# Displacement stage: two buffers of x, the factor in the bank, sums of weights spread, POOL adds the tiles of x

## The reference

```
x = x + mamba(ln_c(x))                      # layer 0
t = to_tokens(x); t = t + ffn(ln_t(t)); x = from_tokens(t)
x = x + displace_and_smooth(ln_c(x), offset) # layer 1
t = to_tokens(x); t = t + ffn(ln_t(t)); x = from_tokens(t)

ln_c(v)  = (v - mean over channels) / sqrt(variance over channels + 1e-6)
ffn(x)   = bitlinear(gelu(bitlinear(x, W1, b1)), W2, b2)
bitlinear: each of 5 groups of rows of W becomes sign(W - mean of the group);
           y is scaled by 128 / (max |y| + 1e-5) for each image and clipped; only the first 5 of 8 images are kept
```

## Time and profile before

| | |
|---|---|
| median of 3 runs | 3997.6 us (3991.24 to 4003.83) |
| the profiled execution | 3997.12 us, its span 3995.3 us |
| PE busy | 3294.7 us, 82% of the span |
| DVE busy | 3593.4 us, 90% |
| ACT busy | 2429.6 us, 61% |
| POOL busy | 2658.3 us, 67% |
| mean granted clock of TensorE | 0.84 |
| displacement, first L1185 to first matmul of the next layer | 3392.03 to 3600.58 us |

### The profile page before, as it was taken

The page is one execution under the profiler, slowest core; times in us unless marked ns, Lnnn a source line. Parts: engine busy times, 40 slices in busy tenths (PEclk is TensorE's granted clock), DMA queues, the critical chain, the costliest instruction groups (busy, mean ns, idle before and its releaser), DMA issues. The chain is left out here.

```text
span 3995.3 us, 46643 instructions
## 1 busy us (share of the span) xinstructions
PE 3294.7 (82%) x12666; PEld 2070.6 (52%) x12666; DVE 3593.4 (90%) x3917; ACT 2429.6 (61%) x4147; POOL 2658.3 (67%) x2119
## 2 busy tenths in 40 slices
PE   5878878787878778787878888788768999788998
PEld 2444444445444444444444444445436777456776
DVE  4999999999999999999999999999957888786786
ACT  4766575676667566655756575676535564575653
POOL 3898988989798888888898988989921110253110
PEclk7878878796878878687878878797779999898999
DMA  3020211202020211202020211202030113452112
GB/s 139 9 101 21 97 61 50 93 17 94 17 100 17 101 51 59 94 17 93 17 101 17 101 43 67 93 17 85 16 103 17 51 62 117 168 189 79 49 49 80
DMA packets 81582, 275.28 MB, mean 69 GB/s; under 512 B 15212, under 2 KB 24044, under 8 KB 64900
## 3 DMA queue, kind: packets, MB, share of 16 engines
q1 hardware_dynamic: 80516, 270.82, 18.5%
q10 hardware_dynamic: 768, 1.05, 0.1%
HBM read 229.90 MB, written 41.95 MB: 68 GB/s over the span
## 5 line engine op out<-in xcount | busy, mean ns | idle before, releaser
L644 POOL TENSOR_TENSOR slot<-dtu,b_rep 128x512 f32<-128x512 f32 x1536 | 1908.3, 1274 | 125.2 <-PE ysum L350 125.0
L350 PE MATMUL ysum<-ident,slot 128*128 128x128 f32 x6144 | 1091.1, 327 | 468.9 <-DVE slot L735 258.3
L535 ACT ACTIVATE state<-dt,aneg 128x512 f32<-128x512 f32 x1536 | 1046.1, 689 | 538.3 <-DVE slot L735 503.0
L350 PEld LDWEIGHTS ysum<-ident,slot 128*128 128x128 f32 x6144 | 854.9, 168 | 930.4 <-DVE slot L735 429.0
L735 DVE TENSOR_TENSOR slot<-state,c_rep 128x512 f32<-128x512 f32 x1248 | 839.0, 673 | 0.0
L727 DVE TENSOR_TENSOR_SCAN state<-state,carry,slot 128x512 f32<-128x512 f32 x624 | 792.3, 1280 | 3.6 <-ACT state L535 3.4
L727 DVE TENSOR_TENSOR_SCAN state<-state,slot 128x512 f32<-128x512 f32 x624 | 755.8, 1221 | 37.8 <-ACT state L535 37.8
L654 POOL TENSOR_TENSOR slot<-slot,c_rep 128x512 f32<-128x512 f32 x288 | 366.1, 1271 | 246.0 <-ACT carry L544 158.0
L544 ACT ACTIVATE carry<-state 128x1 f32<-128x1 f32 x624 | 103.1, 165 | 315.7 <-DVE slot L735 314.9
L1282 ACT ACTIVATE hid<-ph_l,bias_l 128x512 f32<-128x512 f32 x240 | 165.0, 691 | 207.5 <-PE ph_l L1080 206.2
L1080 PE MATMUL ph_l<-xh,w 128*128 128x512 f32 x720 | 216.5, 410 | 31.6 <-DVE xl L1506 11.3
(11 more groups left out here) (214 smaller groups left out, 4975.6 us busy)
## 6 DMA issues: line engine op xcount, KB each, us to landing
b_rep<-rows_of_b_and_c SPq DMA_DIRECT2D x64, 1024.0 KB, 4.7
c_rep<-rows_of_b_and_c SPq DMA_DIRECT2D x64, 1024.0 KB, 4.6
xres_l<-between_layers SPq DMA_DIRECT2D x18, 1536.0 KB, 10.1
xn_l<-between_layers SPq DMA_DIRECT2D x17, 1536.0 KB, 8.5
between_layers<-y SPq DMA_DIRECT2D x10, 1536.0 KB, 6.3
xn<-in_x SPq DMA_DIRECT2D x16, 768.0 KB, 4.4
xres<-in_x SPq DMA_DIRECT2D x16, 768.0 KB, 4.5
between_layers<-xres SPq DMA_DIRECT2D x16, 768.0 KB, 3.5
```

Source lines behind the costliest of these rows:

```text
L350: last = mm(ysum[:, cols], slot[:, (NS * k + n) % SLOTS, cols], ident[:], start=n == 0 and j == 0, stop=n == NS - 1, is_transpose=True, sk ...
L535: af(state[:, (NS * k + n) % BANKS], dt[:, k], ACT.Exp, scale=aneg[:, k, n:n + 1]).then_inc(exp_done, 1)
L644: tt(slot[:, q % SLOTS], dtu[:, k % 2], b_rep[:, n], ALU.mult).then_inc(dbu_done, 1)
```

## The change

1. **Two buffers of x.** `xd` is `xn` for even d and a new place `xn_d` for odd d. `load_d(d)` waits for the centring of d-2, not of d-1. The load of image 1 is issued in the last feed-forward image, once its place is free, and that of image 2 right behind it; the load of W2 moves from in front of them to behind the store of the last feed-forward result.
2. **The factor in the bank.** Exp writes its result into `ph[h]` instead of `rstd`, and `scale_of_d` reads it there. The next mean waits for the scaling (`normed_d`) where it waited for Ln.
3. **Sums of weights spread.** The ten group sums go one by one into d = 1, 2 and 3, behind the centring; the means are made in d = 4; the signs go into d = 4, 5 and 6, behind `read_y`.
4. **POOL adds the three tiles of x.** A new function `sum_tiles_d` on POOL adds the tiles into `xsum_d`, and a mean takes one matmul per half (four records instead of twelve).
5. The mean of image 1 moves from behind the ninth down step of the last feed-forward image to behind the twelfth, and `center_of_d(1)` behind `result_largest`.

```diff
+SUM_IN = ((), (0, 1, 2), (3, 4, 5), (6, 7, 8, 9), (), (), (), ())
+TOTAL_IN = 4
+SIGN_IN = ((), (), (), (), (0, 1, 2), (3, 4, 5, 6), (7, 8, 9), ())
...
+        xsum_d = (xsum[0], put("xsum_d", [P, HW], "shared", 19 * TILE // 2))
...
+        xd = (xn, put("xn_d", [P, CT, HW], "shared", NMAT * (P + 2 * SIDE) * 4))
...
             def load_d(d):
                 if d == 0:
                     sp.wait_ge(split_lo, HALVES * FFN_B)
+                elif d == 1:
+                    sp.wait_ge(down_full, DOWNS - AHEAD + 1)
+                    nc.sync.sem_inc(top_seen, 1)
+                    sp.wait_ge(mean_d, HALVES)
                 else:
-                    sp.wait_ge(centered_d, HALVES * d)
+                    sp.wait_ge(centered_d, HALVES * (d - 1))
...
-            sp.wait_ge(down_full, DOWNS)
-            load_w2(1)
+            load_d(1)
             load_d(2)
             spread_top(LAST[0])
             finish(LAST[0])
             sp.dma_start(xres[:], X[MOVED[0]]).then_inc(xres_in_d, 16)
             for d in range(B):
+                if d == 0:
+                    sp.wait_ge(down_full, DOWNS)
+                    load_w2(1)
                 if d + 3 <= B:
                     load_d(d + 3)
...
             def mean_of_d(d):
-                pe.wait_ge(x_in_d, 16 * (d + 1))
...
-                    pe.wait_ge(ln_read_d, HALVES * d)
+                    pe.wait_ge(normed_d, HALVES * d)
...
+                pe.wait_ge(x_summed_d, d + 1)
                 for h in range(HALVES):
-                    for t in range(CT):
-                        last = mm(ph[h][:], mean_w[:], xn[:, t, half(h)], start=t == 0, stop=t == CT - 1)
-                    last.then_inc(mean_d, 1)
+                    mm(ph[h][:], mean_w[:], xsum_d[d > 0][:, half(h)], start=True, stop=True).then_inc(mean_d, 1)
...
-                    r = rstd[:, half(h)]
-                    af(r, r, ACT.Exp, scale=-0.5).then_inc(rstd_d, 1)
+                    af(ph[h][:], rstd[:, half(h)], ACT.Exp, scale=-0.5).then_inc(rstd_d, 1)
...
                     v.tensor_tensor(xc[:, :, half(h)], xc[:, :, half(h)],
-                                    rstd[:, half(h)].unsqueeze(1).broadcast_to([P, CT, T]), ALU.mult).then_inc(normed_d, 1)
+                                    ph[h][:].unsqueeze(1).broadcast_to([P, CT, T]), ALU.mult).then_inc(normed_d, 1)
...
+            def sum_tiles_d(d):
+                pool.wait_ge(x_in_d[d % 2], 16 * (d // 2 + 1))
+                if d == 0:
+                    pool.wait_ge(mean_full, HALVES * FFN_B)
+                elif d == 1:
+                    pool.wait_ge(down_full, DOWNS)
+                else:
+                    pool.wait_ge(mean_d, HALVES * d)
+                o, a = xsum_d[d > 0], xd[d % 2]
+                tt(o[:], a[:, 0], a[:, 1], ALU.add).then_inc(sum_step_d, 1)
+                pool.wait_ge(sum_step_d, d + 1)
+                tt(o[:], o[:], a[:, 2], ALU.add).then_inc(x_summed_d, 1)
...
+            sum_tiles_d(0)
             pool.wait_ge(up_full, UPS)
             nc.gpsimd.memset(mats[:], 0.0).then_inc(mats_zero, 1)
+            sum_tiles_d(1)
             for d in range(B):
+                if d + 2 <= B:
+                    sum_tiles_d(d + 2)
                 add_moved(d)
```

More of the change, by code:

```diff
@@ L914, in layers @@
         step, tapped, gauss = sem("step"), sem("tapped"), sem("gauss")
-        x_in_d, xres_in_d, stored_d = sem("x_in_d"), sem("xres_in_d"), sem("stored_d")
+        x_in_d, xres_in_d, stored_d = [sem(f"x_in_d{j}") for j in range(2)], sem("xres_in_d"), sem("stored_d")
+        sum_step_d, x_summed_d = sem("sum_step_d"), sem("x_summed_d")
         mean_d, centered_d, squared_d, var_d = sem("mean_d"), sem("centered_d"), sem("squared_d"), sem("var_d")
@@ L1371, in sign1, with sign2 @@
                 af(w1[:, :, group(HID, q)], raw1[:, :, group(HID, q)], ACT.Sign, bias=wmean[:, 0, q:q + 1]).then_inc(signed1, 1)
-            def sign2(layer):
+            def sign2(layer, q):
                 act.wait_ge(means_done, GROUPS + 1 if layer == 0 else GROUPS + 3)
-                for q in range(GROUPS):
-                    last = af(w2[:, :, group(DM, q)], raw2[:, :, group(DM, q)], ACT.Sign, bias=wmean[:, 1, q:q + 1])
-                last.then_inc(signed2, 1)
+                af(w2[:, :, group(DM, q)], raw2[:, :, group(DM, q)], ACT.Sign, bias=wmean[:, 1, q:q + 1]).then_inc(signed2, 1)
             def square_of_d(d, h):
@@ L1432, in _ @@
                 if m == 3:
-                    sign2(0)
+                    for q in range(GROUPS):
+                        sign2(0, q)
                 if m == MEAN_BEFORE:
@@ L1460, in _ @@
                         take_high(FIRST[1], t)
+                for j in SIGN_IN[d]:
+                    if j < GROUPS:
+                        sign1(1, j)
+                    else:
+                        sign2(1, j - GROUPS)
             for m in range(MT):
@@ L1629, in group_sum1, with group_sum2 @@
                 return v.tensor_reduce(wsum[:, 0, q:q + 1], raw1[:, :, group(HID, q)], AX.XY, ALU.add)
-            def group_sum2(layer):
+            def group_sum2(layer, q):
                 dve.wait_ge(w2_in, 16 * (layer + 1))
-                for q in range(GROUPS):
-                    last = v.tensor_reduce(wsum[:, 1, q:q + 1], raw2[:, :, group(DM, q)], AX.XY, ALU.add)
-                last.then_inc(summed, 1)
+                return v.tensor_reduce(wsum[:, 1, q:q + 1], raw2[:, :, group(DM, q)], AX.XY, ALU.add)
             def group_mean1(q):
@@ L1749, in _ @@
                 group_mean1(q)
-            group_sum2(0)
+            for q in range(GROUPS):
+                group_sum2(0, q).then_inc(summed, 1)
             dve.wait_ge(sums_full, GROUPS + 1)
@@ L1774, in _ @@
                 scale_of_d(d + 1)
-                if d == SUM_IN[0]:
-                    for q in range(GROUPS):
-                        last = group_sum1(1, q)
-                    last.then_inc(summed, GROUPS)
-                if d == SUM_IN[1]:
-                    group_sum2(1)
                 if d == TOTAL_IN:
@@ L1785, in _ @@
                         center_of_d(d + 2, h)
+                for j in SUM_IN[d]:
+                    if j < GROUPS:
+                        group_sum1(1, j).then_inc(summed, 1)
+                    else:
+                        group_sum2(1, j - GROUPS).then_inc(summed, 1)
                 if d == 0:
```

32 lines of the change are left out of this document (13 added, 19 removed).

## The result

| | before | after |
|---|---|---|
| median (5 runs each) | 4000.54 us (3991.24 to 4003.83) | 4025.72 us (4019.62 to 4026.8) |
| ratio | | 1.0052, 95% interval 1.0039 to 1.0064 |
| the profiled execution, its span | 3997.12, 3995.3 | 4022.55, 4020.8 |
| DVE busy | 3593.4 | 3571.5 |
| POOL busy | 2658.3 | 2681.7 |

The changed kernel is slower by 25 us, in the medians and in the profiled pair. (The ratio in the table isn't the quotient of these two medians, which is 1.0063; it stands for 21 us, with an interval from 16 to 26.) The forecast was 4012, which is +15. The sign and the mechanism are as predicted, and 4025.72 lies within 3994 to 4036, but outside 4004 to 4020, which had been given 0.6: the cost is some 10 us larger than forecast.

A forecast was written before the change was run, and what follows sets the result against it. No engine is full; a chain through VectorE sets 23.39 us a period, and POOL's sums join it, making 29.0. The steps sum to +16, taken as +15 on 3997.1: 4012, forecast 4004 to 4020 (0.6), range 3994 to 4036.

The forecast's parts named there:

- the wait that decides: PE idle for some 9 us in front of each mean, until POOL's sums behind its add are done.
- step 1: Until image 0's first displacement: 0 change, start at 3392.2, after PE waits 4.9 for POOL's sums of image 1.
- step 2: From there to image 2's first displacement: start at 3449.6, before 3444.4, with x of image 3 landing at 3441.2.
- step 3: Images 2 to 7: five periods of 29.0 against 23.4, image 7 at 3594.6 instead of 3574.0, +20.6.
- step 4: To the next feed-forward layer: last scaling 3.5 shorter, ScalarE waits 0.9 less for a centring, -4.4.
- mean and clock: PE from the mean to the next first displacement: 1.8 for the mean plus 1.8 for the low clock, 3.6.
- W2's 6 us: Load of W2, 2.28 MB, queued ahead of x of image 3, delays that x by 6.0 us more.
- The edits costed at nothing: Spread reductions, PE's new wait for the weights' means, and moved signs: all hidden, 0; uncovered, ten reductions cost 1 each.
- the end of the 13.78: PE's stall of 13.78 for the sums of the weights goes once these are spread.
- The factor in the bank doesn't free POOL: Rival: scaling stays 6.9 and POOL's add 11.6, period 32.1, +37, 4034 us; chance 0.13.
- The clock doesn't fall: Rival: PE keeps its clock, five periods of 27.2, +2.5 or less, about 3998 us; chance 0.12.
- VectorE bounds, not POOL: Rival: POOL's sums fit its idle time, 19.9 a period, -29, 3968 us; chance 0.12.

The follow-up runs named there:

- the second pair: The kernel before and the changed kernel, both unchanged, each profiled once more: 3996.29 and 4022.97 us.
- the extra matmuls: The changed kernel with nine unused matmuls on PE before each mean's wait for POOL's sums: 4024.14 us from image 2 on, 4016.55 us for images 4 to 8 only.

## Why the prediction was right, step by step

The sign, the wait that decides and its length came out as forecast; the size was 10 us short. The changed trace is shifted by 3.9 where the mixer ends (taken at the first instruction behind it on VectorE, 2962.9 before, not at the rough 2950 of the overview); with that taken off, the four steps compare with the forecast like this:

| | forecast | measured, shift taken off |
|---|---|---|
| 1. image 0's first displacement | 3392.2 | 3394.8 |
| 2. image 2's | 3449.6 | 3453.3 |
| 3. five periods | 5 x 29.0 | 5 x 29.6 |
| image 7's | 3594.6 | 3601.3 |
| 4. to the second group of up matmuls, against before | -4.4 | -6.5 |
| whole stage | +16 | +20.7 |
| ahead of it, and behind it | 0 | +3.9, +0.9 |

So the missing 10 are 3.9 ahead of the stage, 2.6 in step 1, 1.1 more in step 2, 3.0 in step 3, 0.9 behind the stage and 1 from rounding +16 down to +15, less the 2.1 of step 4. The prediction asked that the stages ahead keep their length within 3. They didn't, by 3.9, and by 6 in the second pair. The code there is the same and the stage itself grew as forecast, so it isn't a sign that the wrong place was counted, but no step foresaw it.

*Step 1* was 2.6 short. The last down matmuls ended where it said (3383.8 with the shift taken off, forecast 3383.9), but PE waited 7.48 and not 4.9. POOL's sums of image 1 started at 3390.25, when x had landed; the working had costed the sums and not asked when their input comes. It is issued at 3378.11, behind a store and the load of `xres` at 3375.35 and 3375.78.

*Step 2* holds: x of image 3 landed 20.9 behind the store, forecast 20.5, and sums, mean and clock took 8.45, forecast 8.4. The store itself was 3.3 late, 2.6 of it from step 1. The reason given for the landing, W2's 6 us, was confirmed as a delay, but the run with that load moved shows that POOL's add would have held the sums back to 19.3 anyway. I had not looked at that wait.

*Step 3* has the mechanism and, but for the clock, the size. The pieces of the period 3457.18 to 3486.67, forecast in brackets: displacement to ScalarE 1.6 (1.2), from there to `te` 9.5 (9.4), to POOL 1.4 (1.4), add 8.5 (8.5), sums 4.9 (4.9, and 0.1 for the hand-over), mean and clock 3.55 (3.6). The term that was too small is the clock: 2.3 a period where 1.8 was taken, since it stays low into the displacement (L1193 takes 5.91 to 6.66 in four of the five periods instead of 5.34), and ScalarE waits for its first banks.

*Step 4* gave 2.1 more than said. The scaling is 3.5 shorter as forecast; the split in front of the next layer (L1506, 8.24 in the earlier trace rows) was taken as staying slow, and took 6.5 from its first start to its last end, with 1.0 of waiting in it.

*The edits costed at nothing.* The spread sums of the weights cost nothing in the changed kernel, as forecast: PE's matmul of the sums at 3533.91 falls into the wait for POOL, which is even shorter in that period (7.63). But the forecast called the end of the 13.78 a gain that it then didn't book apart, and the run with this edit alone shows that without POOL's cover the means take 11.5 back.

*The rivals.* "The factor in the bank doesn't free POOL" fell: all 18 scalings took 1.72 to 1.75. By the Trainium skill (SBUF — State Buffer, Who interferes with whom) that was to be expected for an instruction with one SBUF input, and this trace agrees. The 16 instructions that the prediction took for its row don't all lie beside a busy POOL, as it says: at the first, at 10.85 us, POOL was idle. The run with the factor in SBUF gave that rival's world, 32.31 a period where it said 32.1, and 43 above the kernel before of its batch where it said +37; the changed kernel came out 10 above its own forecast. "The clock doesn't fall" fell with the windows at 0.50; its period of 27.2 is close to what the extra matmuls gave. (Its own terms add up to +2.5 and so to 3999.6, not 3998.) "VectorE bounds, not POOL" was wrong for this kernel, but gives the period of another one: with POOL's order and the loads changed, four periods are 20 where it said 19.9. That the time agrees too, 3968.85 with its 3968, is luck: in that kernel one period was 6.6 longer, image 2 started 42.5 behind image 0 and not 58.5, since the load of x moved, and the kernel before stood 5 higher in that batch. What decided was, as the prediction had it, POOL's order, and one thing more that it hadn't named, the place of the loads in SP's list.

```profile
L1711 DVE TENSOR_TENSOR hid<-hid,ph_l x18: 1715/1740/1754, 3377.1 to 3620.7; 128x1536 f32<-128x1536 f32 x18
```

## What to carry to other kernels

Work moved to an engine that has idle time is free only if that engine's list lets it run in the idle time: ask what stands ahead of it in the list, when that gets its inputs, and when its own input lands. Here the same two instructions per image cost 31 us behind the add. With the sums one step and the loads one image earlier the kernel is 34 us faster than before, and with the means of the weights ahead of the transposes as well, 45. When an order is changed, look down the chain for the next holder (POOL's add, then the load of x, then VectorE), and change them together: the order alone gave 11 of the 65 us that lie between the changed kernel and the best one.

## What the runs showed of the hardware

- A VectorE product of two SBUF operands and POOL's add slow each other down: 3.4 for one half instead of 1.74, and 11.6 for three tiles instead of 8.6. With one operand in PSUM neither is slowed (1.72 to 1.75, and 8.6); undoing the edit and making it alone both show it.
- After waits of 19.13 and 9.71 PE ran at a granted clock of 0.50 in the two windows of 3.7 that were read, and the mean behind each wait of 7.5 to 19 took 3.54 to 3.75 instead of 1.98. Behind waits of 1.6 to 2.1 the mean took 1.98, and the clock stood at 1.00. In the best version a wait of 3.10, the sum over ten columns and a wait of 0.33 were followed by a mean of 3.78 (granted clock 0.50 from 3495.85 to 3500.35), and a wait of 3.49 at image 3 by one of 3.61. So shorter waits than the prediction's two, 6.92 and 13.78, were followed by the low clock too.
- The issue of the load of x on SP behind a store and two loads of 1.5 and 2.3 MB took 6.76, and 6.7 to 6.9 in every trace that has W2's load right in front of it. With x in front of W2 it took 1.02, and W2's 1.33. What held SP isn't shown; nothing was late for it here, since SP's next instruction waited for POOL.

```profile
3428.83 1.07 SPq L946 DMA_DIRECT2D raw<-in_W2T  x1
3430.01 6.76 SPq L982 DMA_DIRECT2D xn_d<-between_layers  x1
```
